# Log attention: the output addition, the fetched rows, the value copies and the sends placed anew

## The reference

```
L   = q . k * scale ;  L_y = q . k_y * scale                (512 x 512 per head, causal)
agg = sum(exp(clip(L_y, -15, 15)) * mask) + EPS
r   = log(|L| + EPS) - log(agg + EPS)
w   = softplus(r) * mask ;  A = w / (sum(w) + EPS)
x   = x + (A . v) @ w_proj.T
```

```
x = x + shared(x) + w0 * expert_first(x) + w1 * expert_second(x)
```

## Time and profile before

| | us |
|---|---|
| median of 3 runs | 1050.93 (1049.24 to 1052.95) |
| the profiled execution | 1056.77 |
| its span, first to last instruction | 1054.9 |
| TensorE busy in the span | 832.1 (79%) |
| VectorE busy | 744.2 (71%) |
| ScalarE busy | 569.1 (54%) |
| GpSimd busy | 566.7 (54%) |
| mean granted TensorE clock | 0.897 |

### The profile page before, as it was taken

The page is one execution under the profiler, slowest core; times in us unless marked ns, Lnnn a source line. Parts: engine busy times, 40 slices in busy tenths (PEclk is TensorE's granted clock), DMA queues, the critical chain, the costliest instruction groups (busy, mean ns, idle before and its releaser), DMA issues. The chain is left out here.

```text
span 1054.9 us, 19542 instructions
## 1 busy us (share of the span) xinstructions
PE 832.1 (79%) x6459; PEld 551.6 (52%) x6459; DVE 744.2 (71%) x1546; ACT 569.1 (54%) x805; POOL 566.7 (54%) x775
## 2 busy tenths in 40 slices
PE   3788477899986777787878787988786678899890
PEld 2677366799974332333333333333343246799890
DVE  3788844455563669998979798888879736455574
ACT  1444142233334578897887879998764332233230
POOL 2343584881463646565633333334425877788784
PEclk9899787999997799898999899999868579999896
DMA  8990012124337478383726454652210021132434
GB/s 261 300 125 1 18 35 68 51 86 125 99 84 218 141 212 228 118 232 100 218 88 198 123 149 134 189 150 61 80 41 16 32 75 39 38 102 81 131 113 138
DMA packets 114401, 124.00 MB, mean 118 GB/s; under 512 B 13328, under 2 KB 76560, under 8 KB 114176
## 3 DMA queue, kind: packets, MB, share of 16 engines
q1 hardware_dynamic: 96512, 100.80, 35.2%
q0 software_dynamic: 8416, 17.29, 5.4%
q10 hardware_dynamic: 9376, 4.65, 1.5%
HBM read 59.97 MB, written 62.72 MB: 116 GB/s over the span
## 5 line engine op out<-in xcount | busy, mean ns | idle before, releaser
L2067 DVE TENSOR_SCALAR ring_b<-psum 128x1024 int32<-128x1024 int32 x160 | 194.6, 1218 | 35.0 <-PE psum L1762 34.8
L1927 ACT ACTIVATE ring_a<-psum 128x1024 f32<-128x1024 f32 x160 | 162.6, 1021 | 73.9 <-PE psum L1762 72.2
L2210 POOL TENSOR_SCALAR_AFFINE_SELECT ring_b<-ring_b 128x512 f32<-128x512 f32 (+1 forms) x112 | 79.3, 721 | 208.5 <-ACT ring_b L1933 208.3
L1933 ACT ACTIVATE ring_b<-ring_b 128x1024 f32<-128x1024 f32 x160 | 168.8, 1055 | 33.8 <-DVE ring_b L2067 33.5
L1762 PE MATMUL psum<-stacks 32*128 32x128 f32 (+3 forms) x1024 | 100.3, 390 | 65.3 <-DVE ring_b L2067 39.7
L1762 PEld LDWEIGHTS psum<-stacks 32*128 32x128 f32 x1024 | 57.6, 196 | 167.5 <-ACT ring_a L1927 77.1
L2059 DVE TENSOR_SCALAR ring_a<-ring_a 128x1024 f32<-128x1024 f32 x160 | 112.4, 708 | 22.5 <-ACT ring_a L1927 22.5
L1794 PE MATMUL psum<-ring_a,ones_s 128*32 128x256 f32 (+3 forms) x1024 | 94.2, 478 | 15.4 <-ACT delta L1972 8.2
L1815 PE MATMUL psum<-ring_b,values 128*32 128x256 f32 (+3 forms) x1024 | 100.0, 503 | 7.4 <-POOL ring_b L2210 7.4
L949 ACT ACTIVATE ring_b<-psum 128x512 f32<-128x512 f32 x72 | 42.6, 592 | 113.0 <-PE psum L834 113.0
L2210 POOL TENSOR_SCALAR_AFFINE_SELECT ring_a<-ring_a 128x512 f32<-128x512 f32 (+1 forms) x112 | 83.2, 756 | 30.5 <-DVE ring_a L2059 30.4
(11 more groups left out here) (220 smaller groups left out, 1483.6 us busy)
## 6 DMA issues: line engine op xcount, KB each, us to landing
stack_q<-parts SPq DMA_DIRECT2D x32, 256.0 KB
stack_ky<-parts SPq DMA_DIRECT2D x32, 256.0 KB
stacks<-stack_q SPq DMA_DIRECT2D x64, 128.0 KB, 3.0
stacks<-stack_ky SPq DMA_DIRECT2D x64, 128.0 KB, 3.5
stack_k<-parts SPq DMA_DIRECT2D x32, 256.0 KB
stacks<-stack_k SPq DMA_DIRECT2D x64, 128.0 KB, 2.7
stack_qr<-parts SPq DMA_DIRECT2D x32, 256.0 KB
stacks<-stack_qr SPq DMA_DIRECT2D x64, 128.0 KB, 2.5
```

The source lines that it names most:

```text
L1927: nc.scalar.activation(exps[:, n % RING, 2 * u:2 * u + 2, :], psum[:, first:first + 2, :], ACT.Exp, scale=SCALE).then_inc(self.exp, 1)
L1933: nc.scalar.activation(part, part, ACT.Ln, bias=1.0).then_inc(self.ln, 1)
L2067: nc.vector.tensor_scalar(ring[:, m % RING, HEADS_B[u][0]:HEADS_B[u][1] + 1, :].bitcast(I32), psum[:, first:first + 2, :].bitcast(I32), 0x ...
L2210: ins = nc.gpsimd.affine_select(out=part, in_=part, pattern=[[0, part.ap[1][1]], [1, 128]], compare_op=ALU.is_ge, fill=0.0, base=0, channe ...
```

## The change

- The output projection of batch a - 3 moves, still in step 2, ahead of the sums of exponentials on TensorE; `add_output` moves from the first half of step 3 to the second half of step 2 on VectorE.
- `add_choice` adds one tile at a time. In rounds 1 to 5 the eight tiles stand in steps 0, 3, 3, 4, 5, 5, 6, 6 (`FETCHED`); round 0 keeps its places.
- `copy_values` and `correct_counts` move from VectorE to GpSimd, in the same steps 8 and 0, behind the step's masks and ahead of its fetch.
- The second pair of normalised tiles moves on ScalarE from the end of step 0 to the first half of step 2; the table of the lead follows.
- `send` no longer calls `pause`. The pauses in `scatter` and in the early fetches stay.

```diff
-        SCALAR_LEAD = {1: (-11,), 2: (-10,), 3: (-7,), ...}
+        SCALAR_LEAD = {1: (-11,), 2: (-8,), 3: (-7,), ...}
...
                         in_=row, in_offset=None).then_inc(self.sent_soon if c == 0 else self.sent, 16)
-                    pause(p)
...
-            def add_choice(self, v, b, n):
-                if n == 0:
+            def add_choice(self, v, b, n, t):
+                if t == 0 and n == 0:
                     ...
                     v.wait_ge(self.shared_x, self.shared_count(b))
-                else:
+                if t == 0 and n == 1:
                     v.wait_ge(self.first_x, TT * b)
-                for t in range(TT):
-                    at = (b - 1) * TT + t
-                    ins = nc.vector.scalar_tensor_tensor(...)
+                at = (b - 1) * TT + t
+                ins = nc.vector.scalar_tensor_tensor(...)
...
+        FETCHED = {(0, 1): ((0, 0),), (3, 0): ((0, 1),), (3, 1): ((0, 2),), (4, 0): ((0, 3),),
+                   (5, 0): ((1, 0), (1, 1)), (6, 0): ((1, 2), (1, 3))}
+        FETCHED_FIRST = {(4 + n, 0): tuple((n, t) for t in range(TT)) for n in range(2)}
...
@@ tensor_step @@
                 self.scores(pe, n, m, 0)
+                if i == 2 and 0 <= a - 3 < B - 1:
+                    self.project_out(pe, a - 3)
                 if 0 <= n - 2 < STEPS_A:
                     self.sum_exps(pe, n - 2)
                 if i == 0 and 0 <= a - 3 < B - 1:
                     self.pick(pe, a - 3, 1, 0)
-                if i == 2 and 0 <= a - 3 < B - 1:
-                    self.project_out(pe, a - 3)
...
@@ scalar_step @@
+                if i == 2 and 0 <= a + 1 < B:
+                    self.normalise(a_, a + 1, 2)
...
-                if i == 0 and 0 <= a + 1 < B:
-                    self.normalise(a_, a + 1, 2)
...
@@ vector_step @@
-                if i == 0 and 0 <= a - 2 < B:
-                    self.correct_counts(v, a - 2)
...
-                if i == 3 and 0 <= a - 3 < B - 1:
-                    self.add_output(v, a - 3)
-                if i in (4, 5) and ...:
-                    self.previous.add_choice(v, self.previous.first_in_rest - 1 + a, i - 4)
+                self.add_fetched(v, a, i, 0)
...
+                if i == 2 and 0 <= a - 3 < B - 1:
+                    self.add_output(v, a - 3)
                 if i == 2 and 0 <= a - 1 < B:
                     self.split_low(v, "qr", a - 1)
+                self.add_fetched(v, a, i, 1)
...
-                if i == 8 and 0 <= a < B:
-                    self.copy_values(v, a)
...
@@ pool_step @@
                     self.mask(p, exps[:, (n - 1) % RING], (n - 1) % DUS).then_inc(self.mask_a, 1)
+                if i == 8 and 0 <= a < B:
+                    self.copy_values(p, a)
+                if i == 0 and 0 <= a - 2 < B:
+                    self.correct_counts(p, a - 2)
                 if n >= 1:
                     self.previous.late_fetch(p, n - 1)
```

More of the change, by code:

```diff
@@ L547, in build @@
         LEAD_STEPS = 12
-        SCALAR_LEAD = {1: (-11,), 2: (-10,), 3: (-7,), 4: (-6,), 5: (-5,), 6: (-4,), 10: (-1,)}
+        SCALAR_LEAD = {1: (-11,), 2: (-8,), 3: (-7,), 4: (-6,), 5: (-5,), 6: (-4,), 10: (-1,)}
         VECTOR_LEAD = {0: (-12,), 4: (-6,), 5: (-5,), 6: (-4, -3), 9: (-2,)}
@@ L1487, in add_choice @@
                     v.wait_ge(self.shared_x, self.shared_count(b))
-                else:
+                if t == 0 and n == 1:
                     v.wait_ge(self.first_x, TT * b)
-                for t in range(TT):
-                    at = (b - 1) * TT + t
-                    ins = nc.vector.scalar_tensor_tensor(xs(b, t), fetched[:, b % 4, n, t, :], gate[:, n, at:at + 1],
-                                                         xs(b, t), ALU.mult, ALU.add)
-                    if n == 0:
-                        ins.then_inc(self.first_x, 1)
-                if n == 1:
+                at = (b - 1) * TT + t
+                ins = nc.vector.scalar_tensor_tensor(xs(b, t), fetched[:, b % 4, n, t, :], gate[:, n, at:at + 1],
+                                                     xs(b, t), ALU.mult, ALU.add)
+                if n == 0:
+                    ins.then_inc(self.first_x, 1)
+                elif t == TT - 1:
                     ins.then_inc(self.x, 1)
             def add_routed(self, v, b):
-                self.add_choice(v, b, 0)
-                self.add_choice(v, b, 1)
+                for n in range(2):
+                    for t in range(TT):
+                        self.add_choice(v, b, n, t)
             def lead_logits(self, v, k):
@@ L2084, in scale_q @@
                                                ).then_inc(self.q_ready, 1)
-            def copy_values(self, v, b):
-                v.wait_ge(self.v_tok, b + 1)
-                if b == 0:
-                    v.wait_ge(set_values, 2)
-                if b > 1:
-                    v.wait_ge(self.weighted, DUS * (b - 1))
-                for t in range(TT):
-                    room = values[:, b % 2, t, :, :]
-                    dst = bass.AP(room.tensor, room.offset, [room.ap[0], [2 * OW, HALF], [OW + 2 * HD, 2], [1, HD]])
-                    ins = nc.vector.tensor_copy(dst, v_tok[:, b % 2, t, :].rearrange("p (h r d) -> p h r d", r=2, d=HD))
-                ins.then_inc(self.v_ready, 1)
-            def correct_counts(self, v, b):
-                v.wait_ge(self.delta_link, 2 * b + 2)
-                if b > 0:
-                    v.wait_ge(self.emptied, 2 * b - 1)
-                nc.vector.tensor_tensor(delta_n, const["counts"][:], delta[:], ALU.mult).then_inc(self.corrected, 1)
             def correct_values(self, v, b):
@@ L2141, in add_output, with add_fetched @@
                 nc.vector.tensor_tensor(xs(b + 1, 0, TT), bank(7), xs(b + 1, 0, TT), ALU.add).then_inc(self.x, 1)
+            def add_fetched(self, v, a, i, place):
+                b = self.previous.first_in_rest - 1 + a
+                if not self.previous.first_in_rest - 1 <= b <= B:
+                    return
+                for choice, t in (FETCHED_FIRST if a == 0 else FETCHED).get((i, place), ()):
+                    self.previous.add_choice(v, b, choice, t)
             def vector_step(self, v, n):
@@ L2212, in mask, with copy_values, correct_counts @@
                 return ins
+            def copy_values(self, p, b):
+                p.wait_ge(self.v_tok, b + 1)
+                if b == 0:
+                    p.wait_ge(set_values, 2)
+                if b > 1:
+                    p.wait_ge(self.weighted, DUS * (b - 1))
+                for t in range(TT):
+                    room = values[:, b % 2, t, :, :]
+                    dst = bass.AP(room.tensor, room.offset, [room.ap[0], [2 * OW, HALF], [OW + 2 * HD, 2], [1, HD]])
+                    ins = nc.gpsimd.tensor_copy(dst, v_tok[:, b % 2, t, :].rearrange("p (h r d) -> p h r d", r=2, d=HD))
+                ins.then_inc(self.v_ready, 1)
+            def correct_counts(self, p, b):
+                p.wait_ge(self.delta_link, 2 * b + 2)
+                if b > 0:
+                    p.wait_ge(self.emptied, 2 * b - 1)
+                nc.gpsimd.tensor_tensor(delta_n, const["counts"][:], delta[:], ALU.mult).then_inc(self.corrected, 1)
             def pool_step(self, p, n):
```

1 line of the change is left out of this document (removed).

## The result

The changed kernel took 1104.22 us (median of 4 runs, 1102.93 to 1106.43) beside 1051.3 us for the kernel before: the ratio is 1.051, with a 95% interval from 1.048 to 1.055. The forecast was 1022.6. The same file, measured three more times on three different chips, took 1026.7, 1030.9 and 1028.3 us, which is 0.979, 0.983 and 0.980 of the kernel before beside it. The chip of the first measurement isn't recorded. So there are two results to explain: a gain of some 20 us in the attention that is there in every trace of this kernel, and a loss of some 70 us that is there in one measurement of four.

What follows compares the result with a forecast made beforehand. No engine full throughout; attention steps bound by ScalarE, VectorE or the wait for the output addition. 19.5 + 1.4 + 0.8 + 2.5 + 4.1 = 28.3 us takes the median from 1050.9 to 1022.6; range 1009 to 1036.

Steps and rivals of the forecast that it cites:

- Step (1): Attention, steps 2 and 3: output projected and added half a step sooner; step 3 goes from 8.0 to 5.2 us.
- step (3): Steps 8 and 0: value copies and counts product go to GpSimd; 1.4 us over seven rounds, nothing for the product.
- Step (2): Attention rounds: eight adds spread over steps 0 and 3 to 6; 19.5 us together with the earlier output.
- The add of step 0 sits where ScalarE is full: Step 0 of a round: no wait counted for the moved add, up to 2 us once, in round 1, as bound.
- its first rival: Attention adds and GpSimd block each other: adds all take 1.23 us, 11.6 us lost, median 1034; chance 0.12.
- Clips stretched beyond 0.8 us: Sign of a wrong forecast: attention clips beside GpSimd's masks, 708 ns in the mean before, exceed 0.8 us.
- Step (4): ScalarE, steps 0 to 2: two normalised tiles move from step 0 to step 2, and the lead's table follows; 0 us.
- Step (5): Expert layers and attention tail: 128 sends every 1.27 instead of 1.57 us; gains of 0.8, 2.5 and 4.1 us.
- 0 to 3: First expert layer: bounds in us on the 0.8 us gain from unpaused sends.
- 0 to 5: Attention tail and stretch behind it: bounds in us on the 2.5 and 4.1 us gains from unpaused sends.
- sends reach nothing: Rival: the second router's vector chain sets the tail, all 7.4 us of (5) vanish, 1030 us; chance 0.10.
- GpSimd late in step 8: Slower rival: four copies ahead of step 9's masks; 44 us if wholly exposed in eight rounds, median 1067; chance 0.04.

Runs made afterwards that it cites:

- chip 4: Sixth chip measured: changed kernel without pauses behind sends and scatters 1100.0 us; with copies and counts product back on VectorE, sends unpaused, 1091.4; kernel before 1052.3.

## Why the prediction was right and wrong

**Step (1), the output half a step sooner: right.** Step 3 was to fall from 8.0 to 5.2 us and fell to 4.9; no transposes wait for the addition. Undone alone it costs 9.4 us in the medians (1040.3 - 1030.9) and 14.0 in the body of the traces. Steps 0 to 2, which were to stay at 15.9 us, took 16.8, for the reason under step (3).

**Step (2), spread adds: right in size, one place off.** Steps 3 to 6 of round 4 were to take 21.3 us and take 20.1. An add took 583 ns in the mean of the body, not 0.72 us:

```profile
L1490 DVE SCALAR_TENSOR_TENSOR x_res<-r_rows,gate,x_res 128x128 f32<-128x128 f32 x48 | 26.7, 583 | 2.3 <-DMA r_rows<-y_sorted,rows_of 2.3
```

Undone alone the spreading costs 11.2 us in the body and 3.7 in the medians. "The add of step 0 sits where ScalarE is full" was the wrong half: that add is what puts a clip beside the product of counts.

**Step (3), GpSimd's new work: the term 'nothing' for the product was mis-sized.** A copy takes 0.44 us and the product 1.44, together 3.2 us a round and inside the bounds of 1.9 to 3.9:

```profile
L2210 POOL COPY values<-v_tok 128x128 f32<-128x128 f32 x32 | 13.0, 443 | 0.0
...
L2218 POOL TENSOR_TENSOR y_out<-counts,delta 128x512 f32<-128x512 f32 x8 | 11.5, 1438 | 0.0
```

The copies give about 0.25 us a round, near the forecast 0.2, though not in the step named: step 9 takes 4.5 us instead of the 4.7 to 4.9 with the copies on VectorE, and step 8 stays at 5.3. The product's own time is hidden, but it stretches a clip by 1.1 us, and step 1 takes 6.8 us instead of 5.9. The forecast costed the product by GpSimd's idle time alone and not by whom it blocks, although its first rival, adds and GpSimd blocking each other, had the mechanism; it looked at the adds only. "Clips stretched beyond 0.8 us" did stand among its signs of being wrong, but with no price. By the steps, back on VectorE it should give 0.86 us in each of three rounds, 2.6 us, half of the 5 that were expected of that kernel; it gained 0.7 in the median and 1.3 in the body, as its step 6 was 0.8 and 0.5 us longer in two rounds, and the stretch behind the body was 5 us longer in that trace. Why is open.

**Step (4), the moved normalising: nothing speaks against it.** With the counts on VectorE, and so the clip unstretched, steps 0 to 2 of round 4 take 15.9 us, as in the earlier trace rows. It was not undone alone.

**Step (5), unpaused sends: the step that failed.** The period is 1.27 us, as read from the earlier trace rows. What it brings on undisturbed chips is 1.4 us in the old kernel's medians, against 7.4 forecast, and with a ratio of 0.996 to 1.002 that isn't told from nothing. The first scatter does follow the first output (894.92 behind an output that ends at 894.65), and the stretch behind the body is 315.6 us in the mean of ten traces whose second layer is unpaused (312 to 321), on chips without the delay, and 320.6 in four with it paused (318 to 323, the kernel before among them). But TensorE's idle time at the last mask stayed 4.5 to 5.9 us where 2.5 was expected. The mask itself did come sooner, 1.5 us behind the end of the last logarithm where it was 4.7; TensorE ran dry sooner as well, and about half of the wait is now for the logarithm. The forecast had priced that idle time as if the mask alone set it. A gain in the first layer can't be told: the first exponential came at 326.6 to 334.0 us in four traces with that layer paused and at 326.4 to 331.7 in nine with all its sends unpaused. The grave error is the lower bound. "0 to 3", "0 to 5" and "0 to 5" excluded a loss with no reason given: the trace of before holds no long run of transfers without a pause, so it couldn't show what one does to others. The nearest rows were its last three transfers, each 1.27 us behind the other, at a moment when nobody waited. A wait behind every one of 128 transfers was priced as GpSimd's own time and nothing else. The loss in the first measurement, 38.6 us ahead of the body and 29.0 behind, is nine times the 7.4 us that the step was to bring.

**The sum.** On chips without the delay the forecast of 28.3 us saved stands against 19 to 21 measured (1047.6 - 1026.7, 1049.6 - 1030.9, 1048.9 - 1028.3). The difference of 7 to 9 us is about what the sends were to bring: these three medians lie where the rival "sends reach nothing" had them, at 1030, and not at the forecast 1022.6. The attention came out as forecast or better: 20.9 us by parts (1) to (3), and 22 to 23 by the body of these three traces, the stretched clip included. No rival gave the slower side its true cause, and the 0.04 for it had a place that did not come true: GpSimd late in step 8 did not happen, that step kept its length within 0.1 us.

**The profiled execution and the median.** The unchanged file's profiled span was 1022.1, 1026.0 and 1020.1 us where the medians were 1026.7, 1030.9 and 1028.3. Parts below some 5 us can't be read from one trace's total. The lengths of most single steps repeat to 0.02 us, but not of all: in five traces step 6 of round 4 or 5 took 6.1 to 6.2 us instead of 4.9.

## What to carry to other kernels

A wait that looks like padding may be what lets the other engines go on. If the trace of before has no stretch without it, its removal has no lower bound at zero, however small the wait is by itself. Here nearly all of the gain is in the earlier output and the spread adds: with the pauses kept, and the copies and counts left on VectorE, the kernel takes 1027.8 us, 21 less than before, and no other version was clearly faster beside its own kernel before.

When work is moved to an idle engine, ask beside whom it will run, not only whether the engine has time. And a change that measures 5% slower should be measured a second time, on another chip, before its cause is looked for in the code.

## What the hardware showed unexpectedly

- Late starts: up to 27 us between the end of the producing matmul and the start of the waiting engine, only in unbroken runs of unpaused sends and within 6 us behind them (8 to 32 transfers, 1.27 us apart), in the first measurement and on chip 4, in three kernels; not in the unpaused kernels on five other chips, where 100 transfers in a row did no harm. Semaphore events of engines are missing from exactly these three traces (238, 163, 220); in all the others none or one. Of the steps of landings 2430 to 2720 are missing there and 35 to 80 in the others.
- GpSimd's own sends and its waits for their landing are not delayed with the others: the run goes on at 1.27 us, and the marks behind the longer runs (L1062) wait 1.5 us for the landing, as in the traces without the delay (1.4 to 1.7).
- A two-input operation of GpSimd stretches a one-input clip of VectorE from 0.68 to 1.79 us if it starts first, and a mask of GpSimd grows from 0.63 to 1.15 us if the clip does.
- A pause, a memset of 128x256 with a wait for it, costs 0.30 us of GpSimd's time each, over 256 of them.
